# Seven of eight Gram matrices mirrored by VectorE and ScalarE instead of TensorE, in a Perceiver block

## The reference, cut to what matters

```python
x = x + xattn(ctx_1024, layernorm(x), ...)   # linear cross attention, context 8 x 1601 x 512
x = x + attn(layernorm(x), ...)              # kernelised self attention
x = x + ffn(layernorm(x), ...)               # gated experts

def xattn(encoder, decoder, Wq, bq, Wk, bk, Wv, bv, gamma, beta):
    q = decoder @ Wq.T + bq ; k = encoder @ Wk.T + bk ; v = encoder @ Wv.T + bv
    kv  = einsum('bthd,bthe->bhde', k, v)            # 16 heads of 32
    att = einsum('bqhd,bhde->bqhe', q, kv) / sqrt(32)
    return layernorm(att + decoder) * gamma + beta
```

## Time and profile before

| quantity | value |
|---|---|
| median of three runs | 569.11 us |
| the profiled execution | 568.79 us, span 567.1 us |
| PE busy | 559.7 us, 99% of the span |
| DVE, ACT, POOL busy | 60%, 36%, 40% |
| chain that ended last | PE 92% |
| `mirror`, 80 transposes | 10.1 us busy |
| `g_transposes`, 48 transposes | 6.7 us busy |

### The profile page before, as it was taken

How to read it: one execution, slowest core, us unless ns; L and a number is a source line. 1 busy time by engine, 2 the same in 40 slices (tenths; PEclk the granted TensorE clock), 3 DMA queues, 4 the chain that set the end, 5 groups by cost and what they waited for, 6 DMA issues and landing times.

```text
span 567.1 us, 11780 instructions
## 1 busy us (share of the span) xinstructions
PE 559.7 (99%) x4987; PEld 479.2 (85%) x4987; DVE 341.1 (60%) x410; ACT 203.3 (36%) x296; POOL 227.1 (40%) x182
## 2 busy tenths in 40 slices
PE   9989999999999999999999999999999999999997
PEld 6869889898988989887778998978888888888886
DVE  4869655465644456554587557466685457857741
ACT  4625351523535052351561461423341213434220
POOL 2397987573636657359024101103344443000000
PEclk9989999999999999999999999999999999999999
DMA  8554354323422522303560004205824222999501
GB/s 306 177 214 140 149 188 162 97 79 106 148 92 93 166 93 74 112 1 109 180 224 3 13 3 148 76 1 156 226 79 140 79 74 75 200 243 220 153 1 74
DMA packets 31413, 69.12 MB, mean 122 GB/s; under 512 B 6928, under 2 KB 6928, under 8 KB 28432
## 3 DMA queue, kind: packets, MB, share of 16 engines
q1 hardware_dynamic: 31376, 68.58, 39.1%
HBM read 67.39 MB, written 1.18 MB: 121 GB/s over the span
## 4 chain that ended last, share of the span: by engine, by line
PE 92%; DVE 2%; POOL 0%; issue 0%; ACT 0%
PE ps L339 19%; PE ps L341 18%; PE ps L340 18%; PE ps L879 9%; PE ps L903 4%; PE ps L907 4%; PE ps L895 2%; PE ps L890 2%; PE ps L889 2%; PE ps L894 2%; PE ps L956 2%; PE ps L920 2%; PE ps L1202 1%; PE ps L927 1%; PE ps L1185 1%; PE ps L1115 1%
## 5 line engine op out<-in xcount | busy, mean ns | idle before, releaser
L495 POOL TENSOR_TENSOR psum_tmp<-psum_tmp,raw 128x512 f32<-128x512 f32 (+1 forms) x88 | 144.6, 1643 | 31.1 <-DVE lo L1448 22.5
L879 PE MATMUL ps<-hi 128*128 128x256 f32 (+1 forms) x384 | 119.5, 313 | 0.0
L339 PE MATMUL ps<-hi,gh 128*128 128x512 f32 x192 | 75.6, 394 | 0.0
L341 PE MATMUL ps<-hi,gl 128*128 128x512 f32 x192 | 74.9, 390 | 0.0
L340 PE MATMUL ps<-lo,gh 128*128 128x512 f32 x192 | 74.8, 390 | 0.0
L879 PEld LDWEIGHTS ps<-hi 128*128 128x128 f32 x384 | 72.7, 190 | 1.2 <-ACT hi L577 0.8
L548 POOL TENSOR_TENSOR sx<-sx,raw 128x512 f32<-128x512 f32 x32 | 41.0, 1289 | 76.5 <-DVE raw L1816 76.5
L1448 DVE TENSOR_TENSOR lo<-raw,hi 128x2048 fp32r<-128x2048 f32 (+1 forms) x29 | 63.5, 2189 | 10.6 <-ACT hi L569 9.9
L764 ACT ACTIVATE hi<-raw 128x2048 fp32r<-128x2048 f32 x14 | 26.9, 1918 | 86.6 <-PE ps L341 77.2
L339 PE MATMUL ps<-wvh,gh 128*128 128x512 f32 x128 | 51.1, 400 | 0.0
L341 PE MATMUL ps<-wvh,gl 128*128 128x512 f32 x128 | 50.1, 391 | 0.0
(11 more groups left out here) (228 smaller groups left out, 1167.7 us busy)
## 6 DMA issues: line engine op xcount, KB each, us to landing
raw<-in_ctx SPq DMA_DIRECT2D x23, 1024.0 KB, 4.8
raw<-in_ve SPq DMA_DIRECT2D x8, 1024.0 KB, 5.8
raw<-in_oe SPq DMA_DIRECT2D x8, 1024.0 KB, 6.8
wk<-gm_rows SPq DMA_DIRECT2D x8, 512.0 KB, 9.1
g<-gm_rows SPq DMA_DIRECT2D x8, 512.0 KB, 10.2
raw<-in_ctx SPq DMA_DIRECT2D x16, 128.0 KB, 4.0
cb<-in_ctx SPq DMA_DIRECT2D x8, 256.0 KB, 3.3
xres<-in_x SPq DMA_DIRECT2D x1, 1024.0 KB, 9.6
```

The costliest lines, as they stand in the source:

```text
L339: pe.matmul(dst, wh, xh, start=first, stop=False)
L341: return pe.matmul(dst, wl, xh, start=False, stop=last)
L495: pool.tensor_tensor(psum_tmp[0:k, :], (raw[:, 0, :] if t == 1 else psum_tmp[0:k, :]), raw[0:k, t, :], ALU.add).then_inc(ctx_sum, 1)
L879: pe.matmul(dst, hi[:, t, cols], x, start=start and opens, stop=t == CH * ROWS - 1 and closes, skip_group_check=True)
```

## The change

For batches 0 to 6 no transpose runs on PE. DVE transposes the ten blocks of `mir` in 32x32 squares (`flip_low`, seven STREAM_TRANSPOSE instructions, PSUM to `flipped`). A 128x128 block so treated has each square turned but standing in its old place; ACT moves the squares: `turn` is sixteen ACTIVATEs, each from one group of 32 partitions to another, 32 partitions x 320 elements. DVE adds them (`turned_sums`). For the lower part DVE turns six blocks (`flip_up`, four instructions) and ACT moves the squares with sixteen more ACTIVATEs of 32 x 192 (`lower_blocks`). ACT's copies of `mir` go, and the split of G is one copy and one difference of 128x2048 per batch. Batch 7 keeps the old path. The order on ACT is new: `turn` is cut in three pieces between the M copies, and one chunk's high part stands ahead of the last M copy.

```diff
+            def turn(b, ns):
+                if ns.start == 0:
+                    act.wait_ge(flip_done, b * 7 + 7)
+                for n in ns:
+                    src, dst = quarters(n)
+                    ins = act.activation(turned[dst, :, :, src], flipped[src, :, dst].rearrange("p (r s) n -> p r s n", s=2), ACT.Copy)
+                if ns.stop == 16:
+                    ins.then_inc(turn_done, 1)
+            def turn_between_copies(b):
+                turn(b, range(0, 5))
+                m_copy(b - 1, (0,))
+                turn(b, range(5, 10))
+                m_copy(b - 1, (1,))
+                turn(b, range(10, 16))
+                m_copy(b - 1, (2,))
+                ctx_high(b + 1, 1, False)
+                m_copy(b - 1, (3,))
+            def rest_of(b):
+                ctx_high(b + 1, 2, False)
+                ctx_high(b + 1, 3, False)
+                lower_blocks(b)
+                gh_high(b)
...
+            turn_between_copies(1)
+            rest_of(1)
             with act.Fori(2, B - 1) as b:
-                for c in range(1, 4):
-                    ctx_high(b, c, False)
-                cross_rows(b)
                 ctx_high(b + 1, 0, False)
-                m_copy(b - 1)
-                gh_high(b)
+                turn_between_copies(b)
+                rest_of(b)
...
-            products_of(0, True, lambda: mirror(1), lambda: g_transposes(1))
+            products_of(0, True)
             with pe.Fori(2, B - 1) as b:
                 kv_part(b - 2)
                 gram(b, False)
-                products_of(b - 1, False, lambda: mirror(b), lambda: g_transposes(b))
+                products_of(b - 1, False)
...
+            def flip_low(b):
+                dve.wait_ge(gram_mm, b * 4 + 4)
+                if not isinstance(b, int) or b > 0:
+                    dve.wait_ge(lower_done, b)
+                row2, row3, rows01 = by_block(mir[:, 0, :]), by_block(mir[:, 1, :]), by_block(mir[:, 2, :])
+                for dst, src in ((flipped[:, 0:2, :], rows01[:, 0:4:2, :]), (flipped[:, 2, :], rows01[:, 3, :]), (flipped[:, 8, :], rows01[:, 1, :]),
+                                 (flipped[:, 3:5, :], row2[:, 1:3, :]), (flipped[:, 6, :], row2[:, 0, :]),
+                                 (flipped[:, 5, :], row3[:, 2, :]), (flipped[:, 7:10:2, :], row3[:, 1:4:2, :])):
+                    dve.transpose(dst, src).then_inc(flip_done, 1)
...
             sum_copy(0)
+            turned_sums(0)
+            flip_up(0)
...
-            dve.tensor_tensor(gl[:, :, :], g32[:, :, :], gh[:, :, :].bitcast(F32), ALU.subtract).then_inc(gl_done, 3)
+            gl_low(0)
+            ctx_low(2, 0)
...
+            def sums_of(b):
+                flip_low(b)
+                with_tail(b, False)
+                straight_sums(b)
+                sum_copy(b)
+                turned_sums(b)
+                flip_up(b)
+                ctx_low(b + 1, 1)
+                kv_keep(b - 1)
+                ctx_low(b + 1, 2)
+                ctx_low(b + 1, 3)
+                gl_low(b)
```

More of the change, by code:

```diff
@@ L590, in gh_high @@
-            def gh_high(b):
[L591 to L598, removed]
+                act.wait_ge(s_mm, 1)
@@ new lines, in lower_blocks @@
+            def lower_blocks(b, ns=range(16)):
+                if ns.start == 0:
+                    act.wait_ge(upflip_done, b * 4 + 4)
+                for n in ns:
+                    src, dst = quarters(n)
+                    ins = act.activation(low_pairs(dst)[:, :, :, src], upflip[src, :, :, dst], ACT.Copy)
+                if ns.stop == 16:
+                    ins.then_inc(lower_done, 1)
+            def gh_high(b):
+                if isinstance(b, int) and b == 0:
+                    act.wait_ge(q_mm, KC)
+                else:
+                    act.wait_ge(m_mm, b * 4)
+                    act.wait_ge(gl_done, b)
+                act.wait_ge(g_add, b * 6 + 6)
+                act.wait_ge(lower_done, b + 1)
+                act.activation(gh[:, :, :], g32[:, :, :], ACT.Copy).then_inc(gh_done, 1)
@@ L612, in _ @@
             xT_high(0, (2, 3))
-            act.wait_ge(gram_mm, 4)
-            for m in range(3):
-                act.activation(cross[:, m, :], bank[3 + m][:, :], ACT.Copy).then_inc(cr_act, 1)
+            turn(0, range(0, 8))
             ctx_high(1, 0, False)
-            act.wait_ge(gt_mm, 1)
-            act.activation(lower(g32f), mir[:, 0:2, :].rearrange("p m n -> p (m n)")[:, 0:6 * P].rearrange("p (m n) -> p m n", m=3),
-                           ACT.Copy).then_inc(gh_done, 1)
+            turn(0, range(8, 16))
             ctx_high(1, 1, False)
@@ L845, in gram @@
             def gram(b, first, between=None):
-                second = isinstance(b, int) and b == 1
                 for c in range(CH + 1):
@@ L978, in last_kv_part, with products_of @@
                 mm.then_inc(kv_mm, 1)
[L980 to L987, removed]
+            def products_of(b, first):
+                for m in range(KC):
+                    m_part(b, m, first)
             def run_in():
@@ L996, in _ @@
             gram(0, True)
[L997 to L1001, removed]
+            first_queries(range(KC))
             gram(1, False)
-            products_of(0, True, lambda: mirror(1), lambda: g_transposes(1))
+            products_of(0, True)
             with pe.Fori(2, B - 1) as b:
@@ L1084, in _ @@
             turn_sums()
-            mirror(B - 1)
+            last_mirror()
             pe.wait_ge(s_done, 1)
@@ L1483, in turned_sums @@
                 g = last_block(g32f)
[L1484 to L1495, removed]
+                dve.tensor_tensor(g, g, mir[:, 2, 3 * P:4 * P], ALU.add).then_inc(g_add, 2)
@@ L1598, in _ @@
             straight_sums(B - 1)
-            turned_sums(B - 1)
+            last_turned_sums()
             dve.wait_ge(ld_bk, 16)
```

138 lines of the change are left out of this document (69 added, 69 removed).

## The result

The changed kernel takes 593.02 us (median of four runs, 590.97 to 595.28); the kernel before, run beside it, 569.24. The ratio is 1.042, with a 95% interval of 1.038 to 1.046: slower by 23.8 us, where 567.1 was forecast and 578 was the end of the range. The profiled execution took 591.89 us with a span of 590.1, 23.0 more than the span before.

The account below looks back on a forecast made before the run. TensorE, busy in 99% of the span, was taken as the bound. 568.79 - 3.65 (five stages) + 1.6 (batches 0 and 1) = 566.8 profiled, 567.1 as median against 569.11; range 563.7 to 578.

Parts of the forecast that it names:

- Copies in a row overlap by 0.11 ..., so moves start 0.35 apart: ACT's moves in each product stage: 0.46 us each, overlapping like earlier copies, leaving the last M copy 0.37 late.
- the first rival: ACT's moves do not overlap: spacing 0.46, 1.03 lost a stage, 3.4 in batches 0 and 1, 577.7 us; chance 0.16.
- Half clock: Rival: PE's new 1.2 us idle ahead of each kv halves the clock, six times 1.7, 577 us; chance 0.05.
- The start: Batches 0 and 1: early Gram start eaten up, batch 1's turns later, kv at 77.7 against 76.06, a loss of 1.6.
- two more waits behind POOL: Rival in batches 0 and 1: 2.2 us more in the chain, loss 3.8, total 569.3; chance 0.17.
- The chain: Batches 0 and 1: sum copy, turned sums, turns, lower moves, high and low part make the third chunk ready at 56.7, due 54.4.
- The six transposes at the end of a stage: PE's six later transposes before kv: already hidden behind the last M copy, so their removal gives nothing.
- the rival of two passes: DVE's turns take two passes: 1.35 more a stage, 0.62 lost, five times 3.1, 2.95 early, 575.2 us; chance 0.10.
- the 0.03: DVE's seven turns: 0.03 us added per instruction to a plain pass of 1.90, giving 2.10.
- nothing but the M copy was late in batches 3 to 6: Work beside the M copies, such as low parts and lower moves, has cover; a PE wait on a low part would refute.
- the mirror's 1.1 us per stage: PE's ten mirror transposes cost 1.10 us in each of five product stages (batches 2 to 6), 5.5 to be won.
- 32.70 was forecast: Loop period forecast near 32.7 us, against 33.43 before, from a stage gain of 1.10 - 0.37 = 0.73.

Follow-up runs that it names:

- e1: Changed kernel with every move writing the group of 32 partitions it reads, so the result is wrong; 580.61 us, ratio 1.022.
- e2: Changed kernel with the moves in another order, four in a row writing one partition group and reading four; 590.80 us, ratio 1.042.
- e3: Changed kernel with only the start (batches 0 and 1) reordered: third chunk's high part before lower moves, turned sums before sum copy; 586.11 us, ratio 1.030.
- e7: Changed kernel with POOL's running sums over 16 columns instead of 512, leaving the context's row sums out of the result; 586.10 us, ratio 1.030.
- e4: Changed kernel with the last M copy ahead of the context's high part on ACT; 572.95 us, ratio 1.006.
- e5: Changed kernel with the edits of e3 and e4 together; 566.49 us, ratio 0.996 to the kernel before.
- e6: As e5, with three of the sixteen moves put behind the last M copy; 566.95 us, ratio 0.996.
- e8: As e6, with batch 2's first two low parts earlier on DVE, for batch 1 alone; 570.56 us, ratio 1.003.

## Why the prediction was wrong

**The step that failed** is "Copies in a row overlap by 0.11 ..., so moves start 0.35 apart". They start 0.48 apart, shown by the rows after, and e1 and e2 show why: each move changes the group of partitions, and such a move starts only when the one before it is through. The rows that I took the overlap from all run over the full set of partitions, so they could not bear it out. It was the first rival, with a chance of 0.16, and its price in a stage was right: 1.03 lost forecast, 1.15 measured where the clock stayed full.

**Half clock was a rival by itself, and should have been a part of this one.** Only the held moves make a wait of 2.9, and behind long waits the clock fell to 0.50. That adds 6.5 in the loop and 2.0 behind it; with it the rival's 577.7 would have been some 586, and the earlier trace rows showed an idle of 1.98 followed by half clock. Over all profiles: behind an idle of 2.9 the interval to the next kv products was over a us longer than undisturbed in 13 of 20 cases (the changed kernel, e2, e3, e7), behind 1.9 to 2.1 in two of five (e1), behind 0.7 to 1.0 in none of 17 (e4, e5, e6, e8, intervals with no other wait). The windows show the half clock in each of the longer intervals and in none of the others. Why in some and not in others stays open. No run changed the idle alone, so that it is the idle that brings the half clock is argued from this count and not shown.

**The start was under-sized by 7.2** (a loss of 8.8 for 1.6). The chain was named link by link and in order, but each link was too short: POOL held the sum copy, both additions and two low parts (the rival "two more waits behind POOL", at 0.17, which priced 2.2), the lower moves are held as the others are, 0.37 for 0.25, and the stage of batch 1 lost another 2.1 from turns to kv: it takes 13.8, as that of batch 3 does, so this is the held moves again. On paper the chain was already 2.3 late (56.7 for 54.4), so each us by which a link was too short counted in full.

**What held.** The six transposes at the end of a stage gave nothing; the turns run at one pass, which fells the rival of two passes (1.90, the plain pass alone; no run shows the 0.03 that the prediction added for each instruction); nothing but the M copy was late in batches 3 to 6; and the mirror's 1.1 us per stage is there to be won: with the copy in front of the last moves (e6) the period is 32.31, 1.12 below the 33.43 of before. That e4 and e5 come out at 32.65, where 32.70 was forecast, is chance: the forecast had the high part ahead of the copy and moves 0.35 apart, these runs the copy ahead and moves 0.48 apart.

## What to carry to other kernels

An overlap read from rows holds only for instructions like them in partitions too, not in size alone; where work is cut into pieces that move between partition groups, cost each piece at its full length. When work moves to an engine on which a critical copy stands, count what lies ahead of that copy in its queue, and put the copy ahead of everything that nobody waits for yet: here this swap was worth 20 us, and the whole change, in its best order, 2.4. A late copy that lets TensorE idle costs its wait and can cost again in clock, as it did behind 13 of the 20 waits of 2.9 us.

## What the runs showed of the hardware

ScalarE's moves from SBUF to SBUF start 0.36 apart (32x320) or 0.25 (32x192) when they stay within one partition group, and 0.48 or 0.37, their full length, when the group of the input or of the output changes from one to the next. VectorE turns ten fp32 128x128 blocks out of PSUM, in 32x32 squares, in 1.90 us, which is what plain passes over as many columns add up to the earlier trace rows. A 256-column addition of two SBUF tiles takes 0.42 us alone and 1.49 in the mean beside GpSimd's sums.
